# Expert routing: a slot-to-token table built on TensorE, and tiles that fetch their rows by indirect load

## The reference, cut to what matters

```python
xf = layernorm(x).reshape(N, d)                       # N = 1024, d = 512
scores = softmax(xf @ w_gate)                         # 8 experts
weights, idx = top_k(scores, 2)
# every token goes to its two experts
h = xf[token] @ c_fc[expert]                          # 512 -> 2*768
a, g = split(h)
y = (silu(a) * g) @ c_proj[expert]                    # 768 -> 512
out[token] = sum over its two experts of weight * y
x = x + out
```

## Time and profile before

| | |
|---|---|
| median of 3 executions | 2177.83 us (2176.89 to 2182.11) |
| the profiled execution, its own time | 2178.88 us |
| span in the profile, first to last instruction | 2177.1 us |
| mean granted TensorE clock | 0.928 of full speed |
| PE busy | 1943.0 us, 89% |
| PE weight load busy | 1494.0 us, 69% |
| DVE busy | 1338.7 us, 61% |
| ACT busy | 1120.6 us, 51% |
| POOL busy | 125.4 us, 6% |

### The profile page before, as it was taken

One profiled execution on the slowest core, in us unless ns is written; L12 is line 12 of the kernel. 1 busy time (PEld: TensorE's weight loads), 2 busy tenths in 40 slices (PEclk: granted clock), 3 DMA queues, 4 the chain that ended last, 5 costly groups with the idle time before them and its releaser, 6 DMA issues. The chain is left out here.

```text
span 2177.1 us, 31504 instructions
## 1 busy us (share of the span) xinstructions
PE 1943.0 (89%) x10442; PEld 1494.0 (69%) x10442; DVE 1338.7 (61%) x2423; ACT 1120.6 (51%) x1846; POOL 125.4 (6%) x159
## 2 busy tenths in 40 slices
PE   7978983699999499999999999999968989858998
PEld 5647873699999477777777777787747666623443
DVE  5765662699998264536362635354448999839851
ACT  5753320688887244535353535444436666626640
POOL 0000002100000110000000000000000000012220
PEclk9989885899999799999999999999988888779999
DMA  7410005235332421001000101012040000020000
GB/s 262 147 54 1 0 0 222 112 131 205 130 150 89 153 68 49 34 29 34 29 34 29 48 14 48 14 48 92 1 171 1 1 1 1 1 82 0 5 10 25
DMA packets 25896, 137.45 MB, mean 63 GB/s; under 512 B 4066, under 2 KB 4194, under 8 KB 22116
## 3 DMA queue, kind: packets, MB, share of 16 engines
q1 hardware_dynamic: 19588, 116.18, 14.6%
q0 software_dynamic: 6240, 20.45, 2.8%
HBM read 116.17 MB, written 20.45 MB: 63 GB/s over the span
## 5 line engine op out<-in xcount | busy, mean ns | idle before, releaser
L109 PE MATMUL PS<-cT,qs 128*128 128x512 f32 x1152 | 295.6, 402 | 9.0 <-ACT pb L1406 7.0
L109 PE MATMUL PS<-pT,cN 128*128 128x512 f32 x1152 | 270.0, 392 | 1.7 <-DVE pT L1501 1.7
L109 PEld LDWEIGHTS PS<-cT,qs 128*128 128x128 f32 x1152 | 209.3, 189 | 59.9 <-issue 15.1
L109 PEld LDWEIGHTS PS<-pT,cN 128*128 128x128 f32 x1152 | 213.9, 188 | 45.3 <-DVE pT L1501 1.9
L109 PE MATMUL PS<-fw,xgT 128*128 128x384 f32 x1104 | 204.0, 339 | 3.0 <-DVE xgT L1049 3.0
L109 PEld LDWEIGHTS PS<-fw,xgT 128*128 128x128 f32 x1104 | 191.6, 189 | 8.3 <-issue 3.9
L109 PE MATMUL PS<-ws,xT 128*128 128x512 f32 x672 | 182.3, 430 | 6.4 <-DVE ws L563 4.9
L1049 DVE TENSOR_TENSOR fw<-W,fw 128x1536 fp32r<-128x1536 f32 x92 | 159.4, 1755 | 44.9 <-ACT fw L972 44.9
L1496 DVE TENSOR_REDUCE nmax<-PS 128x1 f32<-128x512 f32 x128 | 87.7, 685 | 156.9 <-PE PS L109 156.3
L109 PEld LDWEIGHTS PS<-ws,xT 128*128 128x128 f32 x672 | 138.8, 209 | 46.4 <-issue 11.3
L972 ACT ACTIVATE fw<-W 128x1536 fp32r x92 | 134.2, 1485 | 50.3 <-issue 50.3
(11 more groups left out here) (246 smaller groups left out, 3407.9 us busy)
## 6 DMA issues: line engine op xcount, KB each, us to landing
W<-in_fc SPq DMA_DIRECT2D x8, 3072.0 KB
cT<-in_ctxT SPq DMA_DIRECT2D x16, 768.0 KB, 5.4
raw_pj<-in_proj SPq DMA_DIRECT2D x8, 1536.0 KB, 6.4
ct_in<-in_ctxT SPq DMA_DIRECT2D x16, 768.0 KB
cn_in<-in_ctxN SPq DMA_DIRECT2D x16, 768.0 KB
W<-in_w SPq DMA_DIRECT2D x2, 4096.0 KB, 13.1
routed_x<-zero SPq DMA_DIRECT2D x23, 256.0 KB, 5.4
xg<-routed_x POOLq DMA_DIRECT2D x23, 256.0 KB, 3.2
```

Source lines behind the costliest of these rows:

```text
L109: mm = nc.tensor.matmul(out, lhs(m, s), rhs(n, s), start=(opens and (s, m, n) == terms[0]), stop=((s, m, n) == terms[-1]))
```

## The change

- No zeros are written: the 23 stores of the cosine layer go, and POOL's clearing of `zero` with them, and the wait at the layer's end. `routed_x` goes; a DRAM tensor `normal_x` [1024, 512] takes its place.
- SP stores each tile of `xn` to `normal_x` as it is finished (8 stores of 256 KB), behind the first expert's `fc` load; `proj` of expert 0 is issued behind these, and `fc` and `proj` of expert 1 each behind a wait for expert 0's.
- DVE works out the slots first (before `owner` and `edge`), for both places, and splits each into the number of its tile and the row in it. It makes `token` [128, 16, 24] (the token's number where the tile number matches, zero elsewhere) and `at_row` [128, 16, 128] (1 where the row matches). PE adds up 16 products, out[row, tile] = sum over tokens of at_row x token: the number of the token that stands in each slot, zero where none does. DVE copies it to `index` as integers. Two more constants are loaded for it.
- POOL no longer scatters. It waits until the 8 stores have landed and `index` is there, and issues `gather(0)` and `gather(1)`, each an indirect load of 128 rows; in the second block every later tile's fetch is `gather(s)` in the place of the plain load.
- `owner`, `edge`, `parity` are made behind `index` and `slot`.

The diff, cut to its core:

```diff
@@ cosine_layer
                 sp.dma_start(wqkv, a["wqkv"]).then_inc(s_w12, 16)
-                sp.wait_ge(s_zero, BASE + 1)
-                PER = ET // (NT - 1)
                 with sp.Fori(0, NT - 1) as i:
                     for u in range(2):
                         sp.wait_ge(c_lo, BASE + 2 * i + u + 1)
                         sp.dma_start(cT[:, u], a["ctxT"][2 * i + 2 + u]).then_inc(s_ct[u], 16)
-                    for n in range(PER):
-                        sp.dma_start(xg_d[bass.ds((PER * i + n) * P, P), :], zero[:, :]).then_inc(s_xg0, 16)
-                for n in range(PER * (NT - 1), ET):
-                    sp.dma_start(xg_d[n * P:(n + 1) * P, :], zero[:, :]).then_inc(s_xg0, 16)
-                sp.wait_ge(s_xg0, BASE + 16 * ET)
             def _(pool):
-                nc.gpsimd.memset(zero[:, :], 0.0).then_inc(s_zero, 1)
@@ expert_layer
+        def gather(s):
+            nc.gpsimd.indirect_dma_start(
+                out=xg[:, s % 2, :], out_offset=None, in_=xn_d,
+                in_offset=bass.IndirectOffsetOnAxis(index[:, s:s + 1], axis=0)).then_inc(xg_in[s % 2], 16)
...
                 def _(sp):
                     sp.dma_start(gate[:, :, :], a["gate"]).then_inc(s_gate, 16)
-                    load(sp, 0)
-                    load(sp, 1)
+                    sp.dma_start(rowid[:, :], a["consts"][:, CN_ROW:CN_END]).then_inc(s_row, 16)
+                    sp.dma_start(raw_fc[:, 0], a["fc"][0]).then_inc(s_fc, 16)
+                    for t in range(NT):
+                        sp.wait_ge(s_norm, BASE + t + 1)
+                        sp.dma_start(xn_d[t * P:(t + 1) * P, :], xn[:, t, :]).then_inc(s_xn, 16)
+                    sp.dma_start(raw_pj[:, 0], a["proj"][0]).then_inc(s_pj, 16)
+                    sp.wait_ge(s_fc, BASE + 16)
+                    sp.dma_start(raw_fc[:, 1], a["fc"][1]).then_inc(s_fc, 16)
+                    sp.wait_ge(s_pj, BASE + 16)
+                    sp.dma_start(raw_pj[:, 1], a["proj"][1]).then_inc(s_pj, 16)
...
-                    pool.wait_ge(s_norm, BASE + NT)
-                    pool.wait_ge(e.s_xg0, BASE + 16 * ET)
-                    pool.wait_ge(s_slot, BASE + 2)
-                    for t in range(NT):
-                        for c in range(2):
-                            nc.gpsimd.indirect_dma_start(
-                                out=xg_d, out_offset=bass.IndirectOffsetOnAxis(slot[:, t, c:c + 1], axis=0),
-                                in_=xn[:, t, :], in_offset=None).then_inc(s_scat, 16)
-                    pool.wait_ge(s_scat, 16 * 2 * NT)
+                    pool.wait_ge(s_xn, BASE + 16 * NT)
+                    pool.wait_ge(s_index, BASE + 1)
+                    gather(0)
+                    gather(1)
...
+                    pe.wait_ge(s_token, BASE + 2)
+                    for n in range(2 * NT):
+                        if n % 4 == 0:
+                            pe.wait_ge(s_at, BASE + n // 4 + 1)
+                        mm = nc.tensor.matmul(ps[3][:, 0:ET + 1], at_row[:, n, :], token[:, n, :],
+                                              start=(n == 0), stop=(n == 2 * NT - 1))
+                    mm.then_inc(i_mm, 1)
...
                     ch.link(nc.vector.tensor_scalar(starts[:, :], starts[:, :], float(P), None, ALU.mult))
+                    ch.link(nc.vector.tensor_tensor(place[:, :, :], ...))
+                    for c in range(2):
+                        ch.link(nc.vector.tensor_tensor(pick[:, :, :], place[:, :, :], oh[c][:, :, :], ALU.mult))
+                        ch.link(nc.vector.tensor_reduce(slotf[:, c, :], pick[:, :, :], AX.X, ALU.add))
+                    ch.link(nc.vector.tensor_scalar(tidf[:, :, :], slotf[:, :, :], 1.0 / P, (P - 1) / 2.0 / P,
+                                                    ALU.mult, ALU.subtract))
+                    ch.link(nc.vector.tensor_scalar(tidf[:, :, :], tidf[:, :, :], ROUND, ROUND, ALU.add, ALU.subtract))
+                    ch.link(nc.vector.scalar_tensor_tensor(modf[:, :, :], tidf[:, :, :], -float(P), slotf[:, :, :],
+                                                           ALU.mult, ALU.add))
+                    for c in range(2):
+                        ch.link(nc.vector.tensor_tensor(in_tile[:, :, :], tile_no.unsqueeze(1).to_broadcast(TS),
+                                                        wide(tidf[:, c, :], TS), ALU.is_equal))
+                        nc.vector.tensor_tensor(token[:, c * NT:(c + 1) * NT, :], in_tile[:, :, :],
+                                                wide(rowid[:, P:P + NT], TS), ALU.mult).then_inc(s_token, 1)
+                    for q in range(4):
+                        nc.vector.tensor_tensor(at_row[:, 4 * q:4 * q + 4, :],
+                                                rowid[:, 0:P].unsqueeze(1).to_broadcast(AT),
+                                                wide(modf[:, c, t0:t0 + 4], AT), ALU.is_equal).then_inc(s_at, 1)
+                    ve.wait_ge(i_mm, BASE + 1)
+                    nc.vector.tensor_copy(index[:, :], ps[3][:, 0:ET + 1]).then_inc(s_index, 1)
+                    for c in range(2):
+                        nc.vector.tensor_copy(slot[:, :, c], slotf[:, c, :]).then_inc(s_slot, 1)
...
@@ second block, gpsimd
                 for s in range(ET):
                     if s >= 2:
                         pool.wait_ge(x_mm, BASE + s - 1)
-                    nc.gpsimd.dma_start(xg[:, s % 2, :], xg_d[s * P:(s + 1) * P, :]).then_inc(xg_in[s % 2], 16)
+                        gather(s)
                     if s >= 2:
                         store(s - 2)
```

More of the change, by code:

```diff
@@ L49 @@
 CN_ALL = CN_PICK + 9 * P + 8
+CN_ROW = CN_ALL
+CN_TOKEN = CN_ROW + P
+CN_TNO = CN_TOKEN + NT
+CN_END = CN_TNO + ET + 1
 def constant_table():
-    t = np.zeros((P, CN_ALL), np.float32)
+    t = np.zeros((P, CN_END), np.float32)
     p = np.arange(P)
@@ L70, in constant_table @@
     t[:, CN_PICK + 9 * P:CN_ALL] = p[:, None] % 8 == np.arange(8)[None, :]
+    t[:, CN_ROW:CN_ROW + P] = p[None, :]
+    t[:, CN_TOKEN:CN_TOKEN + NT] = np.arange(NT)[None, :] * P + p[:, None]
+    t[:, CN_TNO:CN_END] = np.arange(ET + 1)[None, :]
     return t
@@ L175, in cosine_layer @@
     x, cn, ps, ones, ident, sem = e.x, e.cn, e.ps, e.ones, e.ident, e.sem
-    s_cn, s_x, s_w12, s_xg0 = e.s_cn, e.s_x, e.s_w12, e.s_xg0
-    wv0, wt0, wqkv, xg_d = e.wv0, e.wt0, e.wqkv, e.xg_d
+    s_cn, s_x, s_w12 = e.s_cn, e.s_x, e.s_w12
+    wv0, wt0, wqkv = e.wv0, e.wt0, e.wqkv
     with ExitStack() as st:
@@ L196, in cosine_layer @@
         xT = sbuf("xT1", [P, DK, P])
-        zero = sbuf("zero1", [P, D])
         ln = Norm(nc, e, "1", sbuf, ps[7], xT)
@@ L207, in cosine_layer @@
         s_w0, s_x2 = sem("s_w0_1"), sem("s_x2_1")
-        s_zero = sem("s_zero1")
         dve = sem("dve1")
@@ L649, in expert_layer @@
     x, cn, ps, ones, ident, sem, W0 = e.x, e.cn, e.ps, e.ones, e.ident, e.sem, e.W0
-    xg_d, yg_d = e.xg_d, e.yg_d
+    xn_d, yg_d = e.xn_d, e.yg_d
     tri = cn[:, CN_TRI:CN_TRI + P]
@@ L661, in expert_layer @@
         owner = sbuf("owner3", [1, ET], I32)
-        s_slot, s_owner = sem("s_slot3"), sem("s_owner3")
-        s_scat = sem("s_scat3", pool_dma=True)
+        index = sbuf("index3", [P, ET + 1], U32)
+        xg = sbuf("xg3", [P, 2, D])
+        s_slot, s_owner, s_index = sem("s_slot3"), sem("s_owner3"), sem("s_index3")
         raw_fc = W0[:, 0:2 * NFC].rearrange("p (u k n) -> p u k n", u=2, k=DK)
@@ L704, in expert_layer @@
             total, tiles, ends, starts = (rbuf(n, [P, NE]) for n in ("total3", "tiles3", "ends3", "starts3"))
-            slotf = rbuf("slotf3", [P, NT])
+            slotf, tidf, modf = (rbuf(n, [P, 2, NT]) for n in ("slotf3", "tidf3", "modf3"))
+            rowid = rbuf("rowid3", [P, CN_END - CN_ROW])
+            at_row = rbuf("at_row3", [P, 2 * NT, P], F32R)
+            in_tile, token = rbuf("in_tile3", [P, NT, ET + 1]), rbuf("token3", [P, 2 * NT, ET + 1], F32R)
             under = rbuf("under3", [1, ET, NE])
             ownf, halff = rbuf("ownf3", [1, ET]), rbuf("halff3", [1, ET])
-            s_gate, g_mm = sem("s_gate3"), sem("g_mm3")
+            s_gate, g_mm, s_row, s_xn = sem("s_gate3"), sem("g_mm3"), sem("s_row3"), sem("s_xn3")
+            s_token, s_at, i_mm = sem("s_token3"), sem("s_at3"), sem("i_mm3")
             s_var, s_rstd, s_norm, s_turn, s_xT = sem("s_var3"), sem("s_rstd3"), sem("s_norm3"), sem("s_turn3"), sem("s_xT3")
@@ L829, in _ @@
                     ch.link(nc.vector.tensor_tensor(
+                        place[:, :, :], ps[2][:, 0:NT * NE].rearrange("p (t e) -> p t e", t=NT),
+                        starts[:, :].unsqueeze(1).to_broadcast(TE), ALU.add))
+                    for c in range(2):
[3 more added lines that the diff above has]
+                                                    ALU.mult, ALU.subtract))
@@ new lines, in _ @@
+                    ch.link(nc.vector.tensor_scalar(tidf[:, :, :], tidf[:, :, :], ROUND, ROUND, ALU.add, ALU.subtract))
```

(24 more changed lines are left out.)

## The result

The changed kernel takes 2205.97 us (median of 4, 2203.40 to 2211.49) against 2178.24 (median of 4) for the one before: ratio 1.0128, 95% interval 1.0105 to 1.0151. The forecast was 2161.6 us, faster.

What follows compares the result with a forecast made beforehand. The hole before the third layer was bound by POOL's 16 scatter stores and the last one's landing, PE idle 32.48 us. First product 16.2 us earlier, other costs 0: from median 2177.83 to 2161.6 us, range 2156.5 to 2168.

Steps and rivals of the forecast that it cites:

- The 21 later fetches: Second block's indirect row fetches: POOL 0.96 instead of 0.54 us, landing 3.9 instead of 3.2, within 7.29 of room; cost 0.
- The rule weighed there: DVE splits beside POOL gathers: by the skill's SBUF rule they would lose up to a gather's length; forecast took no loss.
- the 0.55 of the earlier trace: Layer 4: a DVE operation beside an indirect gather took 0.55 us against 0.56 expected, read as not held up.
- Routing chain: Routing on DVE and PE in place of the scatter: prefix sums at 361.96, index copied at 371.25.
- The block's end: Meeting between the routing block and the second block: one meeting, 0.93 us, to 375.63.
- Rival 1: Routing block's end waits for gathers in flight, or POOL's meeting is slower: 2.9 us later, 2164.5 us; 12%.
- First product: Start of the second block: PE's first expert product at 380.7 instead of 396.93, 16.2 us earlier.
- SP's queue and the cosine layer: Added stores and waits on SP's queue, and 23 stores and POOL's clearing removed from the cosine layer: each cost 0.
- Rival 2: Expert tiles: 21 gathers each stop DVE for 0.96 us, 20.2 lost against 16.2 won, 2181.8 us; 5%.
- rows might land after 7.29: Expert tiles: fetched rows arriving beyond the 7.29 us of room, or half of the DVE loss, leave near no change; 4%.
- Rival 4: PE's clock comes up early through the table's products before the first expert passes: 1.5 us more won, 2160.1 us; 6%.
- What would show it wrong: Profile signs: PE waiting on rows in later tiles, longer DVE splits, or a first ACT split after 380.

Runs made afterwards that it cites:

- e10: Changed kernel with DVE's split of the last quarter of the fc weights made as two halves; 2181.36 us (one execution).
- e7: Changed kernel with three memsets (1.65 us of POOL work) behind the second gather of the routing block; 2206.45 us (one execution).
- e3: Changed kernel with SP's fc weight load held back until the next tile's first quarter of weights is split, some 5 us later; 2165.48 us, ratio 0.9941.
- e5: Kernel before the change with three memsets (about 1.65 us) on POOL ahead of each plain row load from tile 2 on; 2217.28 us (one execution).
- e2: Changed kernel with plain loads of 128 neighbouring rows in place of the second block's indirect fetches (wrong rows); 2165.03 us (one execution).

## Why the prediction was wrong

The sign was wrong, through one step: "The 21 later fetches ... Hidden with 2.2 to spare at the slowest landing shown, 5.1 ... Cost 0." It was priced as 21 equal fetches, without a look at what stands beside each. Measured: 15 fetches at 0, six at 6.9 us, 41.6 in all. Two readings behind it failed:

- *The landing.* The 3.3 to 5.1 of the earlier trace rows are of a layer in which no 3 MB load stands near a fetch. The spread itself was a small sign: the four gathers that began 1.3 to 3.0 us behind two loads of 768 KB landed in 4.2 to 5.1, the eight between 773 and 822 with no load near them in 3.3 to 4.2. In the expert layer each `fc` load of the kernel before came 1.1 to 1.5 us behind a fetch's start; the timeline had both lines. The question to ask was what comes next on the other queue, and by how much the fetch beats it. The margin was 0.58 to 0.97 us, and the fetch became 0.4 us later by the gaps around it and 1.0 to 1.4 longer.
- *The time on POOL.* 0.96 was taken from gathers that met an idle DVE or, in the earlier trace rows, began before DVE's instruction did. The row was read as showing that a gather doesn't hold up DVE, and that came true: DVE's splits take 1752 ns in the median after, 1755 before. The other order, a fetch that begins while DVE is at it, was not in any row looked at, and it takes 1.51 to 2.04 us (14 fetches). The rule weighed there spoke for this. The Trainium skill, SBUF — State Buffer, section Who interferes with whom, says that a DVE instruction with two SBUF inputs contends with a GpSimd instruction that reads SBUF, that the shared ports are an exclusive lock, and that the order of issue decides who blocks. For the order DVE first the runs agree with it (e10: median 1793 to 1051 ns). For the order POOL first the 0.55 of the earlier trace rows shows no wait, but it hardly tests it: a fetch that had to wait ends 0.84 to 0.86 us after its release, and one that meets an idle DVE takes 0.96 to 0.98, so by estimate only its first 0.1 us can be held up, and in the earlier trace rows DVE began 0.38 us into the gather. By this estimate the rule was set aside on a row that tested neither order.

Point by point:

- **Routing chain**: 9.29 us from prefix sums to `index` forecast, 9.00 measured; PE's 16 products were last, as forecast (3.56 against 3.8); POOL's waking 0.87 against 1.00; the gathers 2.43 against 2.45.
- **The block's end**: 0.93 forecast, about 3.1 measured (373.23 to 376.3). Rival 1 held (2.9 later was its price, the measured excess some 2.1), and e7 shows its mechanism.
- **First product**: forecast 16.2 earlier; 15.2 by the profile's clock, 14.2 when counted from the start of the routing. From the last prefix sum it was forecast at 18.7 us and came at 20.8; the block's end makes up the difference.
- **SP's queue and the cosine layer**: 0 forecast. The weights were there in time; ACT's one wait for context is 3.3 after, 3.1 before.
- **Rival 2** had the right side and the wrong mechanism: it let gathers hold up DVE. That rows might land after 7.29 was named with it, but as a loss near 16 us and in one chance of 4% with other things. It was the case that came, at 41.6 us.
- **Rival 4**: the table's products didn't raise the clock; it was 0.50 in all of 368 to 380.
- **The forecast without the six waits**: 2161.6 and the 2.1 of the block's end are 2163.7; e3, where no fetch is caught, took 2165.48. So the rest of the sum held within 2 us.
- **What would show it wrong** named "PE waiting on `xg<-normal_x` in later tiles", and that is what the profile shows.

## What to carry to other kernels

Before making a small, latency-bound transfer slower or later, list the large transfers that other queues issue near it and the margin by which it now comes first: here 0.6 us of margin hid a price of 41 us. The remedy cost one number: let the large load wait for a later event, or issue the small one as soon as its buffer is free. And when a duration is taken from a row, look at what the neighbouring engine was doing in it, and whether it had begun before or after.

## What the runs showed of the hardware that was not expected

- A 256 KB fetch from POOL's queue whose instruction ends 0.5 to 1.1 us behind the issue of a 3 MB load from SP's queue lands with the load, 9.7 to 12.1 us after its own start, plain or indirect; 0.13 to 0.18 us behind, it lands in 3.2 to 4.7. The Trainium skill, DMA: Bandwidth & Descriptors, section SWDGE vs HWDGE vs iDMA, has it that each DMA engine goes round the queues of both kinds in turn. By that one would expect the fetch to land well before the load has ended; the traces of e5 (9.7 to 10.7 us) and of the changed kernel (11.3 to 11.8) disagree for a load of this size. Why is not known.
- An indirect fetch that began while DVE was in a 1.75 us split ended 0.84 to 0.86 us after the split, in all 14 cases of the changed kernel; a plain load in the same place took 0.54 to 0.55 (e2, before).
- A block's end waited for gathers that no instruction waited for (3.99 us from the last gather's start to the next block's work in e7, with 1.7 us of other work on POOL behind it, and 4.06 in the changed kernel without).
